# Six of eight experts of a cross-attention and expert-choice block: both batches' up projection in seven block products instead of eight

## The chip, the core and the metric

The kernel runs on one core of one Trainium2 chip. TensorE (PE, with its weight loads as PEld) multiplies, VectorE (DVE), ScalarE (ACT) and GpSimd (POOL) do elementwise work, SyncE (SP) issues transfers. The metric is device time in microseconds (us) of one execution, the median of three.

## What is computed

```python
x = x + xattn(layernorm(x), ctx, Wq, Wk, Wv, Wo, bo)      # 8 heads, 77 context rows
# then the experts, on layernorm(x); batch n = 2, tokens t = 2048, d = 512, f = 2048, 8 experts
probs = softmax(einsum('ntd,ed->nte', x, gate_w), axis=-1)
g, m = top_k(probs.transpose(0, 2, 1), 512)               # each expert takes 512 tokens of a batch
xin = x[batch_idx, m]
h = gelu(einsum('nekd,edf->nekf', xin, w1))               # the up projection
h = einsum('nekf,efd->nekd', h, w2)                       # the down projection
out = zeros.at[batch_idx, m].add(g[..., None] * h)
x = x + out
```

All of it is float32, so every large product is made of three float32r matmuls on a high and a low part of each operand: high by high, high by low, low by high.

## The kernel before

A first stage (to about 350 us) does attention, the second norm, the gates, and for batch 0 the choice of tokens. The expert stage then goes through 16 columns, one for each batch and expert, in `pe_experts`, `act_experts`, `dve_experts`, `pool_experts` and `sp_experts`. Each engine's order is written out by hand; semaphores tie them. `columns` (L1066 on) unrolls the first two columns and the last and loops over the other 13.

A column has 16 slots f, one for each chunk of 128 hidden units (KF = 16). In slot f PE does `up(f)`, 4 chunks of d by 3 matmuls of 128x512 into bank 4 + f % 2 (L1270 to L1272), and from slot 2 on `down(f - 2)`, 4 token chunks by 3 matmuls into banks 0 to 3 (L1283 to L1285). So slots 0 and 1 hold an `up` alone, and the column ends with three `down` in a row. A slot with both is 24 matmuls. ACT makes the high parts of the weights two slots ahead (L1125, L1129) and the gelu (L1147); DVE makes the low parts (L1181, L1184) and splits the gelu's result (L1200, L1202). At a column's end DVE and ACT scale two chunks of output each (L1236, L1165), and POOL adds the rows to DRAM by four indirect transfers (L1104). POOL gathers the next column's rows (L690) by a copy of their numbers (L680), and PE transposes them in slots 8, 10, 12 and 14 (L1254).

The choice of batch 1's tokens is woven into the first slots: 15 rounds of bisection, each some small DVE work (`dve_round`, L450 to L483) after the slot's split, and a small count on PE (`pe_round`, L489) after the `up` of the slot behind. `ROUNDS_AT` puts them in slots 3 to 15, 19 and 20, counted from the start of the expert stage; slots 16 to 18 (the first three of column 1) have none. Each column but the first is also looked up one column ahead: DVE makes a one-hot tile in slot 1 (`dve_one_hot`, L579), PE multiplies with it in slot 3 (`pe_lookup`, L586).

Of the kernel before, what the change touches and what calls it, by code (L numbers as in the profile page):

```python
# [4 lines left out]

# [7 lines left out]
P = 128  # L13
# [13 lines left out]
TPB = 2  # L27
# [10 lines left out]
def xattn_expert_choice(nc, x, ctx, wq, wk, wv, wo, bo, gate_w, w1, w2, out):  # L38
# [7 lines left out]
    with top:  # L46
        def sb(scope, name, shape, dt=F32):
            return scope.enter_context(nc.sbuf_tensor(name, shape, dt))
# [39 lines left out]
        grec = sb(top, "grec", [P, TPB])
        rows_in = XB[:].rearrange("p b t d -> p (b t) d")
# [3 lines left out]
        thr = sb(top, "thr", [P, E])  # L93
        cand = sb(top, "cand", [P, E, CAND])
        bits = sb(top, "bits", [P, E, CAND])
        kept = sb(top, "kept", [P, E, CAND])
        best = sb(top, "best", [P, E])
        hit = sb(top, "hit", [P, E, CAND, NT], BF16)
        cnt = sb(top, "cnt", [P, E * CAND], BF16)
        above = sb(top, "above", [P, E, NT], BF16)  # L100
        tied = sb(top, "tied", [P, E, NT], BF16)
        chosen = sb(top, "chosen", [P, E, NT], BF16)
        room = sb(top, "room", [P, E])
        chain = sb(top, "chain", [P, E, NT])
        run = sb(top, "run", [P, E, NT])
        run2 = sb(top, "run2", [P, E, NT])
        place = sb(top, "place", [P, E, NT])
        q1 = sb(top, "q1", [P, E, NT])
        q2 = sb(top, "q2", [P, E, NT])
        quarter = sb(top, "quarter", [P, E, NT])  # L110
# [1270 lines left out]
```

## Time and profile before

| | us |
|---|---|
| median of three executions (1815.7 to 1818.9) | 1816.68 |
| the profiled execution | 1814.09 |
| its span | 1812.3 |
| PE busy | 1776.3, 98% |
| PE weight loads busy | 1486.0, 82% |
| DVE busy | 957.6, 53% |
| ACT busy | 674.1, 37% |
| POOL busy | 270.4, 15% |

Matmuls are pipelined: one of 128x512 is listed with 0.39 us, but the next starts 0.23 us behind it, and this pitch is what it costs. The granted clock of TensorE is given as a share of 2.4 GHz; 0.5 is its lower level, 1.2 GHz. The profile's idle column tells how long an engine waited and for whom.

### The profile page before, as it was taken

The page shows a single profiled execution, that of the slowest core. Times are in us where ns is not written, and L with a number is a line of the kernel's source. Part 1 is how long each engine was busy: PE and PEld are TensorE (multiplying, and loading weights), DVE is VectorE, ACT ScalarE, POOL GpSimd, SP SyncE. Part 2 cuts the span into 40 slices and gives each one's busy share as a digit, 9 for nine tenths or more (in the row PEclk, how much of TensorE's full clock was granted, in tenths as well). Part 3 has the DMA queues.
Part 4 walks back from the last instruction along what each step waited for, and adds up shares of the span by engine and source line. Part 5 has one row for each costly group of instructions (what it writes and reads, how often), then busy time and mean ns, then how long its engine had stood idle before and what let it go on. Part 6 is the DMA issues. An engine that isn't in the chain of part 4 may idle for free.

```text
span 1812.3 us, 25364 instructions
## 1 busy us (share of the span) xinstructions
PE 1776.3 (98%) x8790; PEld 1486.0 (82%) x8790; DVE 957.6 (53%) x1910; ACT 674.1 (37%) x1546; POOL 270.4 (15%) x339
## 2 busy tenths in 40 slices
PE   7999999799999999999999999999999999999996
PEld 6799988687888888888888888888888888888885
DVE  5455587777665454545454545454545454444442
ACT  4556565353333333323233333333333333333321
POOL 2123222210202020202020202010111111111101
PEclk9999999899999999999999999999999999999998
DMA  3232434232525252424242525252525252424321
GB/s 122 75 135 93 139 106 175 93 129 93 139 93 140 93 139 93 139 93 139 93 139 93 140 93 148 87 154 79 164 72 168 66 172 64 167 70 161 78 85 24
DMA packets 101413, 205.87 MB, mean 114 GB/s; under 512 B 5204, under 2 KB 5358, under 8 KB 101367
## 3 DMA queue, kind: packets, MB, share of 16 engines
q1 hardware_dynamic: 87031, 171.71, 26.6%
q0 software_dynamic: 14336, 33.56, 9.8%
q8 instruction: 27, 0.44, 0.1%
q14 instruction: 19, 0.16, 0.0%
HBM read 171.70 MB, written 33.55 MB: 113 GB/s over the span
## 4 chain that ended last, share of the span: by engine, by line
PE 95%; DVE 2%; ACT 1%; POOL 1%; DMA 1%; issue 0%; SPq 0%; POOLq 0%; DVEq 0%; ACTq 0%
PE ps L1283 13%; PE ps L1270 13%; PE ps L1272 13%; PE ps L1271 13%; PE ps L1285 13%; PE ps L1284 13%; PE ps L939 4%; PE ps L940 4%; PE ps L941 4%; PE ps L1254 2%; PE ps L921 1%; PE ps L968 1%; PE ps L929 1%; PE ps L913 1%; PE ps L286 1%
## 5 line engine op out<-in xcount | busy, mean ns | idle before, releaser
L1147 ACT ACTIVATE hf<-ps 128x512 f32<-128x512 f32 x256 | 153.1, 598 | 854.8 <-PE ps L1272 854.6
L1200 DVE CAST hh<-hf 128x512 fp32r<-128x512 f32 x256 | 110.3, 431 | 599.2 <-ACT hf L1147 599.2
L1270 PE MATMUL ps<-eTh,w1h 128*128 (+1 forms) x1024 | 404.3, 395 | 0.5 <-issue 0.5
L1283 PE MATMUL ps<-w2h,hh 128*128 128x512 f32 x1024 | 401.4, 392 | 0.0
L1272 PE MATMUL ps<-eTh,w1l 128*128 (+1 forms) x1024 | 399.0, 390 | 0.0
L1285 PE MATMUL ps<-w2h,hl 128*128 128x512 f32 x1024 | 398.9, 390 | 0.0
L1284 PE MATMUL ps<-w2l,hh 128*128 128x512 f32 x1024 | 398.7, 389 | 0.0
L1271 PE MATMUL ps<-eTl,w1h 128*128 (+1 forms) x1024 | 398.6, 389 | 0.0
L1104 POOL DMA_INDIRECT out_dram<-Y,sidx x64 | 105.0, 1641 | 1080.8 <-DVE Y L1236 999.0
L1272 PEld LDWEIGHTS ps<-eTh,w1l 128*128 128x128 f32 x1024 | 192.2, 188 | 40.6
L1285 PEld LDWEIGHTS ps<-w2h,hl 128*128 128x128 f32 x1024 | 192.2, 188 | 40.3
L1283 PEld LDWEIGHTS ps<-w2h,hh 128*128 128x128 f32 x1024 | 192.4, 188 | 39.0
L1284 PEld LDWEIGHTS ps<-w2l,hh 128*128 128x128 f32 x1024 | 192.4, 188 | 38.9
L1270 PEld LDWEIGHTS ps<-eTh,w1h 128*128 128x128 f32 x1024 | 192.5, 188 | 38.6 <-issue 0.8
L1271 PEld LDWEIGHTS ps<-eTl,w1h 128*128 128x128 f32 x1024 | 192.5, 188 | 38.1
L1181 DVE TENSOR_TENSOR w1l<-w_raw,w1h 128x512 fp32r<-128x512 f32 x256 | 175.3, 685 | 30.6 <-ACT w1h L1125 30.5
L1202 DVE TENSOR_TENSOR hl<-hf,hh 128x512 fp32r<-128x512 f32 x256 | 177.4, 693 | 8.8
L1184 DVE TENSOR_TENSOR w2l<-w_raw,w2h 128x512 fp32r<-128x512 f32 x256 | 175.4, 685 | 0.0
L1129 ACT ACTIVATE w2h<-w_raw 128x512 fp32r<-128x512 f32 x256 | 160.1, 626 | 0.0
L1125 ACT ACTIVATE w1h<-w_raw 128x512 fp32r<-128x512 f32 x256 | 160.1, 626 | 0.0
L737 ACT ACTIVATE PR<-ps,nmax 128x77 f32<-128x77 f32 x256 | 78.7, 331 | 40.9 <-DVE nmax L831 40.9
L939 PE MATMUL ps<-AH,xTh 128*128 128x308 f32 (+1 forms) x256 | 80.3, 314 | 1.6 <-DVE AL L300 1.6
(159 smaller groups left out, 1716.0 us busy)
## 6 DMA issues: line engine op xcount, KB each, us to landing
w_raw<-in_L_ffn_w_dram SPq DMA_DIRECT2D x128, 1024.0 KB, 7.2
XB<-in_x_dram SPq DMA_DIRECT2D x16, 512.0 KB, 3.9
XR<-in_x_dram SPq DMA_DIRECT2D x16, 512.0 KB, 3.3
out_dram<-X SPq DMA_DIRECT2D x16, 512.0 KB, 4.6
xn_rows<-XN SPq DMA_DIRECT2D x16, 512.0 KB, 5.4
w_raw<-in_L_xattn_Wq_dram SPq DMA_DIRECT2D x1, 1024.0 KB, 8.3
w_raw<-in_L_xattn_Wo_dram SPq DMA_DIRECT2D x1, 1024.0 KB, 11.4
XB<-xn_rows,gidx POOLq DMA_INDIRECT x64
```

The costliest lines, as they stand in the source:

```text
L1125: nc.scalar.activation(w1h[:, f % SLOTS1], w1_raw[:, g % 2, :, j * P:(j + 1) * P], ACT.Copy).then_inc(f_w1h, 1)
L1129: nc.scalar.activation(w2h[:, f % SLOTS2], w2_raw[:, g % 2, j, :], ACT.Copy).then_inc(f_w2h, 1)
L1147: nc.scalar.activation(hf[:, f % 2, :], ps[:, 4 + f % 2, :], ACT.Gelu).then_inc(f_gelu, 1)
L1181: nc.vector.tensor_tensor(w1l[:, f % SLOTS1], w1_raw[:, g % 2, :, j * P:(j + 1) * P], w1h[:, f % SLOTS1].bitcast(F32), ALU.subtract).then_ ...
L1184: nc.vector.tensor_tensor(w2l[:, f % SLOTS2], w2_raw[:, g % 2, j, :], w2h[:, f % SLOTS2].bitcast(F32), ALU.subtract).then_inc(f_w2l, 1)
L1202: nc.vector.tensor_tensor(hl[:, f % 4], hf[:, f % 2, :], hh[:, f % 4].bitcast(F32), ALU.subtract).then_inc(f_h, 1)
L1270: nc.tensor.matmul(ps[:, 4 + f % 2, :], wh, flat_eTh[:, chunk], start=(k == 0), stop=False)
L1271: nc.tensor.matmul(ps[:, 4 + f % 2, :], wh, flat_eTl[:, chunk], start=False, stop=False)
L1272: last = nc.tensor.matmul(ps[:, 4 + f % 2, :], wl, flat_eTh[:, chunk], start=False, stop=(k == KD - 1))
L1283: nc.tensor.matmul(ps[:, c, :], th, wh, start=(f == 0), stop=False)
L1284: nc.tensor.matmul(ps[:, c, :], th, wl, start=False, stop=False)
L1285: last = nc.tensor.matmul(ps[:, c, :], tl, wh, start=False, stop=(f == KF - 1))
```

## The change

Experts 0 and 1 of both batches (`PLAIN`, four columns, 64 slots) go on as before, all unrolled. For experts 2 to 7 the two batches are done together. The weight block of a group of four f chunks is cut in two halves of d and two halves of f (chunk f = 2q + half), the gathered rows in two halves of d and the two batches; the result's four blocks (half of f, batch) come from seven block products in Winograd's form of Strassen's algorithm instead of eight. A product is done for q = 0 and 1, each time 2 chunks of d by 3 matmuls, so a group has 14 pieces of 6 matmuls, 84 where the same results took 96. Then all 96 matmuls of `down` follow. Six experts by four groups make 24 groups.

What is new beside the matmuls: four sums of weight blocks for each group on POOL (`w_sums`, SS1 to SS4); the high and low part of all seven left factors on ACT and DVE (`w_high`, `w_low`); for each expert four sums of row blocks on DVE (`t_stage`), their high parts on ACT (`t_high`) and low parts on POOL (`t_low`); results that PE accumulates from one product into the next are copied out between (`keep_u1`, `keep_u2`, `keep_u7` on ACT) and added on DVE (`c11`, `c22`, `c21`). Gelu is run twice for each chunk, once written as the high part and once in full (`hidden`), in place of DVE's cast. The output of a group is scaled and added to SBUF by DVE alone (`evict`), and POOL adds an expert's eight chunks to DRAM in its last group (`scatter_pair`). Buffers of the plain columns shrink from 4, 8 and 4 to 3, 5 and 3 slots. All tiles get fixed addresses. The rounds of batch 1 stand in slots 3 to 17, and all lookups in slots 24, 26, ... 50, the one-hot tile each time one slot ahead. The gather takes the row numbers directly, without a copy.

```diff
+        PLAIN = (0, 1, E, E + 1)
+        NPE = len(PLAIN) // B
+        LOOKUPS = PLAIN + tuple(b * E + e for e in range(NPE, E) for b in range(B))
...
-        SLOTS1, SLOTS2 = 4, 8
...
+        S1, S2, S3 = 3, 5, 3
...
+        A11, A12, SS2, SS3, SS1, A22, SS4 = range(NPR)
+        B11, B21, TT2, TT3, TT1, TT4, B22 = range(NPR)
+        ALPHA, BETA, GAMMA = (4, 7), (5, 0), (6, 1)
+        CHAIN = {A11: ALPHA, SS2: ALPHA, SS1: ALPHA, SS4: ALPHA, A12: BETA, SS3: GAMMA, A22: GAMMA}
+        OPENS = (A11, A12, SS3)
+        PRODUCTS = ((A11, 0), (A12, 0), (A11, 1), (A12, 1), (SS2, 0), (SS3, 0), (SS2, 1), (SS1, 0), (SS3, 1),
+                    (SS1, 1), (A22, 0), (SS4, 0), (A22, 1), (SS4, 1))
+        NU = len(PRODUCTS)
+        HIDDEN = ((0, 0), (0, 2), (1, 1), (1, 3), (0, 1), (1, 0), (0, 3), (1, 2))
...
+        W_ORDER = (A11, A12, A22, SS1, SS2, SS4, SS3)
...
+        T_AT = (54, 56, 58, 60)
...
-        ROUNDS_AT = tuple(q for q in range(3, 5 + KF) if not KF <= q < KF + LOOKUP)[:ROUNDS]
...
+        ROUNDS_AT = tuple(range(3, 3 + ROUNDS))
         CHOICE_AT = ROUNDS_AT[-1] + 1
-        assert len(ROUNDS_AT) == ROUNDS
...
+        HOT_AT = {1: 1, **{m: VALS_AT + 1 + 2 * (m - 2) for m in range(2, len(LOOKUPS))}}
+        FOUND_AT = {1: 3, **{m: VALS_AT + 2 + 2 * (m - 2) for m in range(2, len(LOOKUPS))}}
...
+            def w_sums(n):
...
+                a11, a12, a21, a22 = (w_block(n, i) for i in (A11, A12, -1, A22))
+                pool.tensor_tensor(Wf[:, SS1], a21, a22, ALU.add).then_inc(s_sum, 1)
+                pool.wait_ge(s_sum, 4 * n + 1)
+                pool.tensor_tensor(Wf[:, SS2], Wf[:, SS1], a11, ALU.subtract).then_inc(s_sum, 1)
+                pool.wait_ge(s_sum, 4 * n + 2)
+                pool.tensor_tensor(Wf[:, SS4], a12, Wf[:, SS2], ALU.subtract).then_inc(s_sum, 1)
+                pool.tensor_tensor(Wf[:, SS3], a11, a21, ALU.subtract).then_inc(s_sum, 1)
...
+                if g == G - 1:
+                    for j in range(ND):
+                        scatter_pair(x, j)
+                        if x + 1 < NS and j in (3, 5):
+                            t_low(x + 1, j // 2 - 1)
...
+                nc.scalar.activation(hhS[:, b, f], src, ACT.Gelu)
+                nc.scalar.activation(hfS[:, b, f], src, ACT.Gelu).then_inc(s_gelu, 1)
...
+            def keep_u2(n, q):
+                act.wait_ge(s_prod, NU * n + 5 + 2 * q)
+                nc.scalar.activation(u2[:, q], ps[:, ALPHA[q], :], ACT.Copy).then_inc(s_u2, 1)
...
+            def group(n):
+                x, g = divmod(n, G)
+                w2_high(n, (0, 1))
+                keep_u1(n, 0)
+                w2_high(n, (2,))
+                hidden(n, 0)
+                keep_u1(n, 1)
+                hidden(n, 1)
+                keep_u2(n, 0)
+                w2_high(n, (3,))
+                keep_u7(n, 0)
+                keep_u2(n, 1)
+                hidden(n, 2)
+                keep_u7(n, 1)
+                for m in range(3, len(HIDDEN)):
+                    hidden(n, m)
...
+            def c11(n, q):
+                dve.wait_ge(s_prod, NU * n + 2 + 2 * q)
+                dve.wait_ge(s_u1, 2 * n + q + 1)
+                nc.vector.tensor_tensor(hfS[:, 0, 2 * q], ps[:, BETA[q], :], u1[:], ALU.add).then_inc(s_c11, 1)
...
+            def product(n, m):
+                idx, q = PRODUCTS[m]
+                x, g = divmod(n, G)
+                bank = CHAIN[idx][q]
+                if q == 0:
+                    pe.wait_ge(s_Wl, NPR * n + W_ORDER.index(idx) + 1)
...
+                if idx == SS2:
+                    pe.wait_ge(s_u1, 2 * n + q + 1)
+                if idx == SS1:
+                    pe.wait_ge(s_u2, 2 * n + q + 1)
+                if idx == A22:
+                    pe.wait_ge(s_u7, 2 * n + q + 1)
+                if idx == SS4:
+                    pe.wait_ge(s_c22, 2 * n + q + 1)
+                go_on = dict(skip_group_check=idx not in OPENS)
+                for k in range(2):
+                    wh, wl = Wh[:, idx, k, q, :], Wl[:, idx, k, q, :]
+                    th, tl = Th[:, idx, k, :], Tl[:, idx, k, :]
+                    nc.tensor.matmul(ps[:, bank, :], wh, th, start=(idx in OPENS and k == 0), stop=False, **go_on)
+                    nc.tensor.matmul(ps[:, bank, :], wh, tl, start=False, stop=False, **go_on)
+                    last = nc.tensor.matmul(ps[:, bank, :], wl, th, start=False, stop=(k == 1), **go_on)
+                last.then_inc(s_prod, 1)
...
+            def group(n):
+                x, g = divmod(n, G)
+                for m in range(NU):
+                    product(n, m)
+                for j in range(2):
+                    for t in range(GF - 1):
+                        down_chunk(n, j, t)
+                for j in range(2):
+                    down_chunk(n, j, GF - 1)
+                for j in range(2, ND):
+                    if g == G - 1 and x + 1 < NS and 2 <= j < 6:
+                        t_stage(x + 1, j - 2, T_BANKS[j % 2])
+                    for t in range(GF):
+                        down_chunk(n, j, t)
```

DVE around the start of column 1. Ahead of the rows stands the work of slot 15; L1236 is the scaling that ends column 0. Before, slots 16, 17 and the first of 18:

```order
L1236 TENSOR_SCALAR Y<-ps,tok_gate 128x512 x2
L1181 TENSOR_TENSOR w1l<-w_raw,w1h 128x512
L1184 TENSOR_TENSOR w2l<-w_raw,w2h 128x512
L1200 CAST hh<-hf 128x512
L1202 TENSOR_TENSOR hl<-hf,hh 128x512
L1181 TENSOR_TENSOR w1l<-w_raw,w1h 128x512
L1184 TENSOR_TENSOR w2l<-w_raw,w2h 128x512
L1200 CAST hh<-hf 128x512
L1202 TENSOR_TENSOR hl<-hf,hh 128x512
L579 TENSOR_TENSOR hot<-row,col_iota 128x2048
```

The same place in the changed kernel, slot 16 alone:

```order
L1609 TENSOR_SCALAR Y<-ps,tok_gate 128x512 x2
L1419 TENSOR_TENSOR w1l<-w_raw,w1h 128x512
L1422 TENSOR_TENSOR w2l<-w_raw,w2h 128x512
L1436 CAST hh<-hf 128x512
L1438 TENSOR_TENSOR hl<-hf,hh 128x512
L466 SCALAR_TENSOR_TENSOR kept<-ps,cand 128x24
L469 TENSOR_REDUCE best<-kept 128x8
L471 TENSOR_TENSOR thr<-thr,best 128x8
L491 TENSOR_TENSOR cand<-thr,bits 128x24
L494 TENSOR_TENSOR hit<-probs,cand 128x384
L496 TENSOR_SCALAR bits<-bits 128x24
L499 TENSOR_REDUCE cnt<-hit 128x24
```

The round that stood in slot 19 has moved to slot 16, and the one of slot 20 to slot 17, which reads the same.

ACT in two slots of the last column before, with what it waits for:

```order
L1125 ACTIVATE w1h<-w_raw 128x512 [waits f_up,f_raw1]
L1129 ACTIVATE w2h<-w_raw 128x512 [waits f_down]
L1147 ACTIVATE hf<-ps 128x512 [waits f_h,f_up]
L1125 ACTIVATE w1h<-w_raw 128x512 [waits f_up]
L1129 ACTIVATE w2h<-w_raw 128x512 [waits f_down]
```

ACT at the start of a group in the changed kernel (u_162 is u1, u_161 u2, u_163 u7; s_prod is PE's count of products, s_c11 and s_c22 are DVE's sums):

```order
L1327 ACTIVATE v2h<-w_raw 128x512 [waits s_dn,s_raw2_0]
L1327 ACTIVATE v2h<-w_raw 128x512
L1355 ACTIVATE u_162<-ps 128x512 [waits s_c11,s_prod]
L1327 ACTIVATE v2h<-w_raw 128x512
L1345 ACTIVATE hhS<-hfS 128x512 [waits s_c11]
L1346 ACTIVATE hfS<-hfS 128x512
L1355 ACTIVATE u_162<-ps 128x512 [waits s_c11,s_prod]
L1345 ACTIVATE hhS<-hfS 128x512 [waits s_c11]
L1346 ACTIVATE hfS<-hfS 128x512
L1350 ACTIVATE u_161<-ps 128x512 [waits s_prod]
L1327 ACTIVATE v2h<-w_raw 128x512
L1360 ACTIVATE u_163<-ps 128x512 [waits s_c22,s_prod]
```

ACT now hands PE operands in the middle of the up projection, behind sums of DVE; before, it stood two slots ahead of PE with the weights and behind it with the gelu.

## Rows read from the trace of the kernel before

**Rows 1.** The page: busy us, share of the span and instructions

```profile
PE 1776.3 (98%) x8790; PEld 1486.0 (82%) x8790; DVE 957.6 (53%) x1910; ACT 674.1 (37%) x1546; POOL 270.4 (15%) x339
```

**Rows 2.** Timeline of PE, one slot (start us, us, engine, line, tiles): first `up` matmuls

```profile
1202.24 0.39 PE L1270 MATMUL ps<-eTh,w1h 128*128 x1
...
1207.68 0.39 PE L1270 MATMUL ps<-eTh,w1h 128*128 x1
```

**Rows 3.** Groups by form: busy us, mean ns, idle before and its releaser

```profile
L1202 DVE TENSOR_TENSOR hl<-hf,hh 128x512 fp32r<-128x512 f32 x256 | 177.4, 693 | 8.8
L1147 ACT ACTIVATE hf<-ps 128x512 f32<-128x512 f32 x256 | 153.1, 598 | 854.8 <-PE ps L1272 854.6
L1104 POOL DMA_INDIRECT out_dram<-Y,sidx x64 | 105.0, 1641 | 1080.8 <-DVE Y L1236 999.0 <-issue 81.8
L706 POOL TENSOR_TENSOR PR<-PR,srec 128x616 f32<-128x616 f32 x32 | 38.9, 1217 | 29.7 <-DVE srec L822 29.5
```

**Rows 4.** Timeline of PE at one of the 60 places of four transposes

```profile
1699.94 0.60 PE L1254 MATMUL ps<-ident,XB 128*128 128x128 f32 x4
1700.30 0.48 PE L1270 MATMUL ps<-eTh,w1h 128*128 x1
```

**Rows 5.** Timeline of ACT and DVE in a slot with a round: gelu, split, round

```profile
426.37 0.60 ACT L1147 ACTIVATE hf<-ps 128x512 f32<-128x512 f32 x1 [4.43 <-PE ps L1272]
427.00 0.43 DVE L1200 CAST hh<-hf 128x512 fp32r<-128x512 f32 x1 [1.80 <-ACT hf L1147]
...
428.07 0.18 DVE L450 SCALAR_TENSOR_TENSOR kept<-ps,cand 128x24 f32<-128x24 f32 x1
...
429.50 0.55 DVE L483 TENSOR_REDUCE cnt<-hit 128x24 bf16<-128x384 bf16 x1
```

**Rows 6.** Timeline at the start of column 1: gelu of slots 16 and 17, `up` of slot 18

```profile
460.71 0.60 ACT L1147 ACTIVATE hf<-ps 128x512 f32<-128x512 f32 x1 [0.99 <-PE ps L1272]
...
463.59 0.60 ACT L1147 ACTIVATE hf<-ps 128x512 f32<-128x512 f32 x1 [1.24 <-PE ps L1272]
...
463.39 0.39 PE L1270 MATMUL ps<-eTh,w1h 128*128 128x512 f32 x1
```

**Rows 7.** Timeline of DVE: the one-hot tile

```profile
555.54 2.28 DVE L579 TENSOR_TENSOR hot<-row,col_iota 128x2048 bf16<-128x2048 bf16 x1
```

**Rows 8.** Windows: us, busy of PE, PEld, DVE, ACT, POOL, granted clock, DMA

```profile
340.00:345.00 5.00, 5.00 (x12) 3.96 (x13) 2.87 (x6) 0.00 (x0) 0.00 (x0) 0.51 0.29 108
```

**Rows 9.** Timeline of PE in attention: the idle time at 340, two matmuls

```profile
339.88 0.77 PE L939 MATMUL ps<-BH,pTh 128*128 128x512 f32 x1 [3.02 <-DVE X L810]
...
346.93 0.39 PE L939 MATMUL ps<-BH,pTh 128*128 128x512 f32 x1
...
349.03 0.40 PE L939 MATMUL ps<-BH,pTh 104*128 104x512 f32 x1
```

**Rows 10.** Timeline of POOL at the first gather, and two powers behind it

```profile
346.97 0.19 POOL L680 COPY gidx<-tok_idx 128x4 uint32<-128x4 uint32 x1 [14.48 <-DVE tok_gate L601]
348.25 1.22 POOL L690 DMA_INDIRECT XB<-xn_rows,gidx  x1 [1.09 <-issue]
...
353.69 0.72 POOL L671 TENSOR_TENSOR rs<-ve,pow_c 128x2 f32<-128x2 f32 x1
...
356.86 1.23 POOL L671 TENSOR_TENSOR rs<-ve,pow_c 128x2 f32<-128x2 f32 x1
```

**Rows 11.** Timeline of DVE behind the first gather

```profile
356.85 0.69 DVE L1181 TENSOR_TENSOR w1l<-w_raw,w1h 128x512 fp32r<-128x512 f32 x1 [1.88 <-ACT w1h L1125]
```

**Rows 12.** Timeline of the kernel's end

```profile
1796.57 1.41 DVE L1236 TENSOR_SCALAR Y<-ps,tok_gate 128x512 f32<-128x512 f32 x2 [4.42 <-PE ps L1285]
...
1798.11 0.39 PE L1285 MATMUL ps<-w2h,hl 128*128 128x512 f32 x1
1798.12 1.57 POOL L1104 DMA_INDIRECT out_dram<-Y,sidx  x1 [70.60 <-DVE Y L1236]
...
1803.73 1.56 POOL L1104 DMA_INDIRECT out_dram<-Y,sidx  x1 [0.31 <-issue]
```

More of the change, by code:

```diff
@@ L100, in xattn_expert_choice @@
[L100 to L110, printed above, removed]
@@ new lines, in xattn_expert_choice @@
+        run = lookup("run", [P, E, NT])
+        run2 = lookup("run2", [P, E, NT])
+        place = lookup("place", [P, E, NT])
+        q1 = lookup("q1", [P, E, NT])
+        q2 = lookup("q2", [P, E, NT])
+        quarter = lookup("quarter", [P, E, NT])
+        row = lookup("row", [P, B, E, NT])
+        rest1 = lookup("rest1", [P, E, NT])
+        rest2 = lookup("rest2", [P, E, NT])
+        gp = [lookup(f"gp{i}", [P, E, NT], BF16) for i in range(3)]
+        inq = lookup("inq", [P, E, NT, CT], BF16)
@@ new lines, in xattn_expert_choice @@
+        W_SUMS = {SS1: 1, SS2: 2, SS4: 3, SS3: 4}
+        W_SUMS_READ = {SS1: 2, SS2: 3, SS4: 3, SS3: 4}
+        D_BANKS = (2, 3, 0)
+        ND = B * CT
+        F_ORDER = ((0, 2, 1, 3), (1, 3, 0, 2))
+        T_SUMS = (TT2, TT3, TT1, TT4)
+        T_BANKS = ((5, 6), (7, 1))
+        T_AT = (54, 56, 58, 60)
+        s_raw1 = [sem(f"s_raw1_{i}") for i in range(2)]
+        s_raw2 = [sem(f"s_raw2_{i}") for i in range(2)]
+        (s_prod, s_u1, s_c11, s_u2, s_u7, s_c22, s_c21, s_gelu, s_hid, s_sum, s_Wh, s_Wl, s_v2h, s_v2l, s_dn, s_ev, s_tr, s_Ta,
+         s_T2, s_Td, s_Th, s_Tl, s_rows, s_scat) = (sem(f"s_{n}") for n in (
+             "prod u1 c11 u2 u7 c22 c21 gelu hid sum Wh Wl v2h v2l dn ev tr Ta T2 Td Th Tl rows scat").split())
@@ L1168, in act_experts @@
             act.wait_ge(p_o, NBLK)
-            for f in range(2):
-                weights(0, f, None, None)
+            for n in range(2):
+                weights(n)
             for k in range(KD):
@@ L1173, in act_experts @@
             act_xn2T(act, NBLK - 2)
-            columns(act, body)
+            for n in range(NPL):
+                slot(n)
+                if n % KF == KF - 1:
+                    i = n // KF
+                    if i:
+                        act.wait_ge(f_scat, 16 * CT * i)
+                    for c in range(CT // 2, CT):
+                        if c < CT - 1:
+                            act.wait_ge(f_out, i * (CT - 1) + c + 1)
+                        else:
+                            act.wait_ge(f_down, n + 1)
+                        nc.scalar.activation(Y[:, c, :], ps[:, c, :], ACT.Copy,
+                                             scale=tok_gate[:, PLAIN[i], c:c + 1]).then_inc(f_ya, 1)
@@ L1246, in pe_experts @@
+            for n in range(NG):
+                group(n)
         def pe_experts(pe):
@@ L1324, in pe_experts @@
             pe_xn2T((NBLK - 2) % 2)
-            columns(pe, body)
+            for n in range(NPL):
+                slot(n)
+            for n in range(NG):
+                group(n)
         with nc.Block() as block:
```

938 lines of the change are left out of this document (630 added, 308 removed).

## The prediction

> **What bounds the kernel now.** I read the busy shares first: PE is busy 98% of the span, the next engine 53% [rows 1]. Then the timeline of PE: a slot of 24 matmuls takes from 1202.24 to 1207.68, 5.44 us, so a matmul of 128x512 costs 0.2267 us [rows 2], though it is listed with 0.39. The expert stage has 6144 such matmuls, 1392.7 us of the span; the rest of PE's time there is transposes, lookups, rounds and gates. ACT waited 854.6 us for PE's `up` [rows 3]. So PE's instruction count sets the time, and a change pays by the matmuls that it takes away, as long as nobody makes PE wait.
>
> **What it removes.** For six experts and both batches the up projection had 2304 matmuls; 24 groups by 84 are 2016. 288 fewer at 0.2267 [rows 2] is **-65.3 us**, all on the path. The down projection keeps its 1152. The Trainium skill (TensorE: Matmul & The Clock Gate, Back-to-back issue gap) gives N / 2.4 + 2.5 ns, 215.7 ns for 512 columns; by it the term would be -62.1, but the row has 226.7 and I keep the row. A group then takes 180 x 0.2267 = 40.8 us where the same work took 43.5.
>
> **Transposes.** Before, 60 places of four cost 0.36 us and 0.08 more in the matmul behind, 0.44 each [rows 4], 26.4 us. After, 12 such places and 24 of eight, about 0.87 each by the same rows doubled without the restart (4 more transposes are 0.36): 26. **0**, between -2 and +2.
>
> **The seven products: does PE wait in a group?** Let t = 0 be a group's first product; product m of the fourteen starts at 1.36 m. A result can be used 0.20 us after its matmul's pitch ends (ACT starts at 463.59 where PE went on at 463.39 [rows 6]). ACT's operation is 0.60 and the next starts 0.5 behind it; DVE's is 0.69 with 0.6 between starts [rows 3, 5]. The waits that PE has in the middle, and when they are met:
> The third pair needs u1: ACT copies it by 2.2 and 5.3; wanted at 5.44 and 8.16. SS1 with q = 0 (wanted at 9.52) needs u2: the fourth product ends at 5.44, DVE's c11 ends at 6.33, ACT's two gelus of chunk (0, 2) start at 6.4 and 6.9, the copy starts at 7.4 and ends at 8.0. That is the tightest link, **1.5 us of slack**. u2 for q = 1 is there at 10.3, wanted at 12.24; u7 at 9.0 and 13.4, wanted at 13.6 and 16.3 (q = 1, 2.9 of slack); c22 at 11.8 and 14.5, wanted at 14.96 and 17.68. The split hidden chunk that the first `down` rows need last is there at 20.4, wanted at 23.1. Behind it DVE makes three low parts and evicts the first bank at 24.7; `down` wants it at 27.2. The other low parts follow POOL's sums. A POOL sum of 512 elements I take as 1217 x 512 / 616 = 1.01 us [rows 3], four in a row from t = 19.2, so the last weight is ready by 30, and it is wanted at 47. Load in a group: ACT some 37 operations by 0.52, DVE 37 by 0.62, 19 and 23 us of 40.8. So **0** for 24 groups. Cover is the 1.5 us; if the chain ran 2 us later, each group would lose 1.
>
> **Change of expert (five times).** In the fourth group of an expert DVE gets 14 operations more and ACT 16, between the evictions. `t_stage` 1 ends on DVE at about 33.8, and PE's fourth set of transposes wants it at 35.3. POOL does `t_low` between scatters of 1.6 us [rows 3]; the second set ends 1 to 4 us into the next group, where its four results are wanted at 5.4, 6.8, 9.5 and 13.6. I take 0 and keep up to 3 us each, +15, as the other end. What could push it there: POOL slows beside DVE. A power of two elements takes 0.72 alone and 1.23 when DVE runs subtractions with both inputs in SBUF [rows 10, 11]. By that ratio (1.7) the four sums would take 7 us, and the set would still be there by 4, 6, 7 and 9. The Trainium skill (GPSIMD Engine Reference, Key points) says that GpSimd contends with VectorE's instructions that have two SBUF inputs, and the trace agrees by those two rows.
>
> **New waits in the plain columns.** Slots 16, 17, 32, 33, 48 and 49 are an `up` alone, 2.72 us. Before, no round stood in slots 16 to 18. Now DVE does one in 16 and 17, and PE's count behind the next `up` waits for it. From the gelu's start to DVE's split is 0.63, the split 1.07, the round 1.98 [rows 5]. Slot 16: the gelu starts at 460.71 [rows 6], the count is ready at 464.45, PE had been done with `up` at 463.39: **1.06**. Slot 17: DVE goes on at 464.32 with two weights (1.2), split and round until 468.63; PE is done at 467.22: **1.41**. What hides the same work elsewhere is the `down` of 2.72 us. The one-hot tile of 2.28 us [rows 7] stood in a column's slot 1 with the lookup two slots on; now slots 33 and 49 make one and PE looks up in 34 and 50: 0.20 + 0.63 + 1.07 + 2.28 + 0.06 = 4.24 after the end of `up`, against one `up` of 2.72: **1.5**, twice. Queued behind PE's wait there is `down`, and its loss is not given back. Together **+5.5**. If the clock fell each time it would cost more: at 340, after 3.02 us of idle, the granted clock was 0.51 (the level of 1.2 GHz) and 11 matmuls ran at 0.43 instead of 0.23 [rows 8, 9], 2.2 us; four times is +9. The gaps here are half as long and lie between full work; I take none.
>
> **Smaller buffers.** Three w1, five w2 and three hidden slots make ACT wait for the `up` one slot back and the `down` three back, both past when it gets there. 0, up to +2.
>
> **The first gather.** The copy at 346.97 and its wait go; the first transfer starts at 348.25 [rows 10]. PE waited 6.1 us for those rows, and POOL's norm stands behind them, so it all moves by about **-1.0** (0 to -1.3).
>
> **The end.** PE's last matmul ends at 1798.50; then come four scatters of 1.57 at a pitch of 1.87, the last from 1803.73 to 1805.3, and 7.0 more to the span's end [rows 12]. After, seven of eight are gone by then: 0.07, the eviction 0.75, 0.8 to POOL's start (as from 1797.32 to 1798.12), 1.57, 7.0: 10.2 instead of 13.8, **-3.6** (-2 to -4.5).
>
> **Addresses.** Every tile moves. No row prices an address. The nearest rows are the same matmul form at two pitches: 0.2267 in the experts and, for no reason that the trace shows, 0.2333 in attention (346.93 to 349.03 for nine [rows 9]). The new products are as the experts' in all else; I take 0, the other end is 5856 x 0.0067 = +39.
>
> **Sum.** 1814.1 (the profiled execution, 1.8 over its span) - 65.3 - 3.6 - 1.0 + 5.5 = 1749.7. It was 2.6 below the median of the runs shown, so I forecast **1752** for the median.
>
> **Rivals.** (1) The change of expert is late, by POOL or by DVE's five operations in a stage: 1 to 3 us, five times, and the four clock falls: 1759 to 1770. For it, three engines in a ring and order fixed; against it the slack above. (2) The pitch of 0.2333 holds in runs of six and three matmuls, as in attention's runs of fifteen: 1752 + 39 = 1791. Against it, `down` before also changed bank every three matmuls, at 0.2267. (3) **Slower than before**: in each group PE stops at SS1's wait for u2. It decides from 65.3 / 24 = 2.7 us per group, so the chain of c11, two gelus and copy must run 4.2 us later than worked out, twice its length. Once PE idles 3 us the clock falls: 3 + 2.2 us, 24 times, +125: 1877. For it: ACT and DVE now stand between PE's own products, and ACT has its queue of 16 gelus; against it: both are half idle. (4) The new waits don't show, since DVE runs ahead: 1746 or a little less.
>
> **Chances.** Forecast (1747 to 1758) 0.68; (4) below 1747 0.08; (1) 0.13; (2) or part of it 0.06; (3) 0.04; another way of no gain 0.01. The range leaves out the last three and half of (4): 1745 to 1768. Below a change of 0.2% a measurement of this kernel can't tell one: faster 0.95, same 0.01, slower 0.04.
>
> **What would show it.** Right: 24 stretches of about 40.8 us with PE at 98% or more and no wait of `product` on ACT or DVE in the list of waits; four waits of PE for DVE's count and one-hot tile, 1 to 1.5 us each; one scatter behind the last matmul; clock at 1.0 from 365 on. Wrong: `product` or `down_chunk` waiting in every group, a pitch of 0.2333 in the groups, the transposes of an expert change waiting for DVE, or POOL's sums at 2 us and more with low parts waited for.

## The result

| | before | changed |
|---|---|---|
| median (4 executions each) | 1816.19 | 1784.94 |
| span of the profiled execution | 1812.3 | 1783.9 |

The ratio is 0.9824, with a 95% interval of 0.9812 to 0.9836: 31 us (1.8%) faster. I had forecast 1752, in a range of 1745 to 1768, so about half of the gain that the sum promised didn't come, and the time lies above the range. The head of the changed kernel's page:

```profile
span 1783.9 us, 22943 instructions
PE 1724.9 (97%) x8502; PEld 1435.8 (80%) x8502; DVE 1164.5 (65%) x1946; ACT 807.7 (45%) x1786; POOL 477.3 (27%) x451
```

PE's busy share fell from 98% [rows 1] to 97%, and DVE's rose to 65%. To see where the time is I cut both traces at the first `up`, at the first product (before: the first `up` of column 4, at 727.14) and at the end of the last matmul:

| stretch, us | before | changed | forecast for the changed |
|---|---|---|---|
| to the first `up` | 361.84 | 362.26 | 360.8 |
| four plain columns | 365.30 | 382.69 | 379.0 |
| 24 groups (before: 12 columns) | 1071.35 | 1027.71 | 997.9 |
| from there to the span's end | 13.84 | 11.27 | 10.2 |

The two stretches of the kernel before, as windows (length, then busy time and instructions of PE, PEld, DVE, ACT, POOL, granted clock, DMA):

```profile
361.84:727.14 365.30, 365.29 (x1724) 299.58 (x1725) 216.84 (x457) 126.73 (x226) 40.02 (x37) 1.00 0.36 114
727.14:1798.49 1071.35, 1071.35 (x4961) 885.55 (x4959) 518.66 (x887) 350.44 (x641) 134.88 (x116) 1.00 0.37 113
```

The forecast for the plain columns holds the 5.5 of new waits and 8.2 that only move there from the later columns. Of these, 6.5 are 11 lookups at 0.59 each: a later column takes 89.47 in the mean, 87.04 for its 384 matmuls, 1.84 for four places of transposes, and the lookup the rest. The other 1.7 are the first joint expert's transposes in sets of eight.

29.8 of the 36.0 us between the forecast's span (1747.9) and the measured one lie in the groups. Four windows of the changed kernel, each exactly one group (engines' busy time and instructions, the granted clock behind `POOL busy`, then DMA): a plain group, the last of an expert, and the first groups of two experts.

```profile
786.35:827.71 41.36, 41.10 (x182) 33.70 (x181) 25.81 (x33) 18.06 (x33) 6.25 (x4) 1.00 0.15 51
869.10:913.47 44.37, 44.37 (x213) 37.09 (x212) 33.93 (x47) 25.83 (x48) 19.50 (x13) 1.00 0.33 72
913.47:958.19 44.72, 41.66 (x181) 33.55 (x180) 30.81 (x33) 18.45 (x35) 25.36 (x19) 1.00 0.48 118
1257.14:1304.32 47.18, 44.52 (x182) 35.43 (x180) 30.83 (x33) 18.55 (x35) 25.33 (x19) 0.93 0.45 111
```

The five last groups of an expert with their transposes take 44.37, no wait in them: 40.80 and four times 0.89. But plain groups take 41.36 instead of 40.80, and the first group of each new expert (five of them) takes 44.72, 44.72, 47.18, 45.52 and 44.72. The sums: the five first groups are 22.9 over five times 40.80, and the 13 other groups with a small gap 7.6 (0.54 to 0.60 each, one 0.85). Together that is 30.5, and transposes that cost 0.6 less in all than I had put (see "Why the prediction was wrong") give the 29.8 within 0.1. Who PE waited for (us in total, times, longest):

```profile
PE ps L1746 <- ACT u L1355: 9.2, 5, 1.9
PE ps L505 <- DVE cnt L499: 4.5, 7, 1.2
PE ps L1746 <- ACT u L1350: 3.8, 5, 0.9
PE ps L1768 <- DVE YS L1546: 3.4, 12, 0.6
PE ps L604 <- DVE hot L596: 3.3, 2, 1.7
```

L1746 is the first matmul of a product piece, L1355 and L1350 are `keep_u1` and `keep_u2`: five times each, once for every change of expert. L1768 is `down` of the group's fourth output chunk, which needs the bank that DVE's first eviction frees (L1546 here; in an expert's first group L1542, six times 0.3 at most). L604 and two of L505 are the new waits in the plain columns.

**The change of expert, read backwards.** Timelines of group 4, the first of the second joint expert (it starts at 913.47), PE, ACT, DVE and POOL (start, length, operation, idle time before it and what ended it):

```profile
921.41 0.39 PE L1748 MATMUL ps<-Th,Wl 128*128 128x512 f32 x1
923.65 0.50 PE L1746 MATMUL ps<-Th,Wh 128*128 128x512 f32 x1 [1.85 <-ACT u L1355]
...
921.96 0.63 ACT L1345 ACTIVATE hhS<-hfS 128x512 fp32r<-128x512 f32 x1 [5.71 <-DVE hfS L1513]
...
923.02 0.58 ACT L1355 ACTIVATE u<-ps 128x512 f32<-128x512 f32 x1
...
914.76 6.57 DVE L1507 TENSOR_TENSOR v2l<-w_raw,v2h 128x512 fp32r<-128x512 f32 x2 [0.34 <-ACT v2h L1327]
921.25 0.68 DVE L1513 TENSOR_TENSOR hfS<-ps,u 128x512 f32<-128x512 f32 x1
...
914.55 5.62 POOL L1209 TENSOR_TENSOR Tl<-Tf,Th 128x512 fp32r<-128x512 f32 x4
```

PE goes on when ACT has copied u1 (923.02 + 0.58). ACT copies behind the two gelus of c11. c11 (L1513) starts at 921.25, 7.8 us into the group; its inputs were there at 916.4 (two products of 1.36 into the group, and 0.2). Ahead of it in DVE's queue stand two low parts `v2l`, together 6.57 us instead of 1.3. The first of them alone is listed with 5.97: it starts 0.2 us behind POOL's four subtractions of `t_low` and ends 0.55 us behind the last of them. The whole kernel by shape (count, busy us, mean ns):

```profile
L1502 DVE TENSOR_TENSOR Wl<-w_raw,Wh 128x512 fp32r<-128x512 f32 x72 | 99.0, 1426 | 0.0
L1507 DVE TENSOR_TENSOR v2l<-w_raw,v2h 128x512 fp32r<-128x512 f32 x96 | 90.4, 962 | 56.8 <-ACT v2h L1327 56.8
L1502 DVE TENSOR_TENSOR Wl<-Wf,Wh 128x512 fp32r<-128x512 f32 x96 | 61.7, 678 | 0.0
...
L1209 POOL TENSOR_TENSOR Tl<-Tf,Th 128x512 fp32r<-128x512 f32 x48 | 69.4, 1839 | 55.8 <-ACT Th L1305 55.8
L1204 POOL TENSOR_TENSOR Wf<-w_raw 128x512 f32<-128x512 f32 x24 | 41.7, 1736 | 0.0
...
L1201 POOL TENSOR_TENSOR Wf<-Wf,w_raw 128x512 f32<-128x512 f32 x24 | 39.0, 1626 | 1.9
```

The same subtraction of 128x512 takes DVE 678 ns behind POOL's sums and 1426 in the mean beside them. **The plain group's gap** is the same thing in small (DVE, then POOL, then PE):

```profile
809.17 4.08 DVE L1502 TENSOR_TENSOR Wl<-w_raw,Wh 128x512 fp32r<-128x512 f32 x3
813.17 1.40 DVE L1546 SCALAR_TENSOR_TENSOR YS<-ps,tok_gate,YS 128x512 f32<-128x512 f32 x2
...
808.78 1.62 POOL L1203 TENSOR_TENSOR Wf<-w_raw,Wf 128x512 f32<-128x512 f32 x1
810.36 1.74 POOL L1204 TENSOR_TENSOR Wf<-w_raw 128x512 f32<-128x512 f32 x1
...
813.97 0.50 PE L1768 MATMUL ps<-v2h,hhS 128*128 128x512 f32 x1 [0.26 <-DVE YS L1546]
```

Three low parts take 4.08 instead of 2.0 while POOL sums, the eviction behind them (813.17) is late, and PE starts its next `down` 0.65 behind the last matmul instead of 0.23. The eviction comes 26.8 into the group, where I had 24.7.

**The plain columns** show the four waits of the forecast, at the places named:

```profile
463.73 0.39 PE L1641 MATMUL ps<-eTh,w1l 128*128 128x512 f32 x1
465.36 0.19 PE L505 MATMUL ps<-cnt,ones_bf 128*128 128x24 bf16 x1 [1.24 <-DVE cnt L499]
...
563.66 0.56 PE L604 MATMUL ps<-vals,hot 128*128 128x20 bf16 x16 [1.68 <-DVE hot L596]
...
565.83 0.63 PE L1652 MATMUL ps<-w2h,hh 128*128 128x512 f32 x1
```

Over the pitch they are 1.40, 1.27, 1.83 and 1.83. Behind each lookup the clock also fell to 0.5, the level of 1.2 GHz, for 3.41 us (565.83 is a matmul of 0.63 there), and 7 and 6 matmuls ran at 0.427: 2.6 us more.

### The profile page after: what moved, and what is told of

Its sections match the earlier page's. It is cut to its first block, busy times and chain, and to the rows that moved or that the text cites. A ratio compares the mean times of both kernels' runs of the same rounds, so it can differ in the third digit from the quotient of the medians.

```text
span 1783.9 us, 22943 instructions
## 1 busy us (share of the span) xinstructions
PE 1724.9 (97%) x8502; PEld 1435.8 (80%) x8502; DVE 1164.5 (65%) x1946; ACT 807.7 (45%) x1786; POOL 477.3 (27%) x451
## 4 chain that ended last, share of the span: by engine, by line
PE 77%; DVE 9%; ACT 7%; issue 6%; DMA 1%; POOL 1%; SPq 0%; DVEq 0%; ACTq 0%; POOLq 0%
PE ps L1746 7%; PE ps L1748 7%; PE ps L1747 7%; PE ps L1768 7%; PE ps L1769 7%; PE ps L1770 7%; PE ps L1652 3%; PE ps L1654 3%; PE ps L1653 3%; PE ps L1639 3%; PE ps L1641 3%; PE ps L955 3%; PE ps L1640 3%; PE ps L956 3%; PE ps L957 3%
## 5 line engine op out<-in xcount | busy, mean ns | idle before, releaser
L1768 PE MATMUL ps<-v2h,hhS 128*128 128x512 f32 x768 | 302.6, 394 | 4.9 <-DVE YS L1546 3.4
L1769 PE MATMUL ps<-v2l,hhS 128*128 128x512 f32 x768 | 299.1, 390 | 0.0
L1770 PE MATMUL ps<-v2h,hlS 128*128 128x512 f32 x768 | 299.0, 389 | 0.0
L1746 PE MATMUL ps<-Th,Wh 128*128 128x512 f32 x672 | 264.0, 393 | 13.0 <-ACT u L1355 9.2
L1748 PE MATMUL ps<-Th,Wl 128*128 128x512 f32 x672 | 263.1, 392 | 0.0
L1747 PE MATMUL ps<-Tl,Wh 128*128 128x512 f32 x672 | 263.1, 392 | 0.0
L1529 DVE TENSOR_TENSOR hlS<-hfS,hhS 128x512 fp32r<-128x512 f32 x192 | 172.3, 906 | 73.9 <-ACT hfS L1346 73.9
L1546 DVE SCALAR_TENSOR_TENSOR YS<-ps,tok_gate,YS 128x512 f32<-128x512 f32 x144 | 105.8, 745 | 113.7 <-PE ps L1770 113.7
L1768 PEld LDWEIGHTS ps<-v2h,hhS 128*128 128x128 f32 x768 | 144.2, 188 | 41.4 <-DVE YS L1546 8.4
L1746 PEld LDWEIGHTS ps<-Th,Wh 128*128 128x128 f32 x672 | 127.0, 189 | 44.0 <-ACT u L1355 11.3
L1652 PE MATMUL ps<-w2h,hh 128*128 128x512 f32 x256 | 103.4, 404 | 0.0
L1654 PE MATMUL ps<-w2h,hl 128*128 128x512 f32 x256 | 101.1, 395 | 0.0
L1653 PE MATMUL ps<-w2l,hh 128*128 128x512 f32 x256 | 101.1, 395 | 0.0
```

The source lines that it names most:

```text
L1529: nc.vector.tensor_tensor(hlS[:, b, f], hfS[:, b, f], hhS[:, b, f].bitcast(F32), ALU.subtract).then_inc(s_hid, 1)
L1546: nc.vector.scalar_tensor_tensor(out=YS[:, j], in0=src, scalar=gate, in1=YS[:, j], op0=ALU.mult, op1=ALU.add).then_inc(s_ev, 1)
L1652: nc.tensor.matmul(ps[:, c, :], th, wh, start=(f == 0), stop=False)
L1653: nc.tensor.matmul(ps[:, c, :], th, wl, start=False, stop=False)
L1654: last = nc.tensor.matmul(ps[:, c, :], tl, wh, start=False, stop=(f == KF - 1))
L1746: nc.tensor.matmul(ps[:, bank, :], wh, th, start=(idx in OPENS and k == 0), stop=False, **go_on)
```

## The experiments

The theory, A: a DVE operation whose operands lie in SBUF alone stands still while POOL runs an elementwise operation, for as long as POOL's operations follow each other; what is queued behind it on DVE (c11, an eviction) carries this to PE. The rivals: B, ACT is late at the change of expert, by its four copies for `Th`; C, DVE's queue there is simply too long.

**1. DVE's low parts of the second layer behind the sums.**

```diff
-                w2_low(n, (0, 1))
                 c11(n, 0)
-                w2_low(n, (2,))
+                c11(n, 1)
+                w2_low(n, (0, 1, 2))
                 low(n, 0)
-                c11(n, 1)
                 w2_low(n, (3,))
```

> The changed kernel with one edit in the order of DVE: the low parts of the second layer's weights (v2l) stand behind the two sums c11, not ahead of them. Theory A: an operation of DVE with both inputs in SBUF stands still while POOL runs its four subtractions for Tl back to back (v2l listed with 5.97 us instead of 0.68 at 914.76), and c11 is queued behind it. c11 has one input in PSUM and isn't held, so PE's two waits in the first group of an expert (2.02 and 1.11 us) and the clock falls behind them go: group 4 from 44.72 to 41.4, groups 12 and 16 from 47.2 and 45.5 too, 1785 to about 1765. One v2l still shows 3 to 5 us. Rival B: ACT is late (its four copies for Th end at 914.2, its copy of u1 starts at 915.16): then DVE's order changes nothing, 1784 to 1786, and group 4 stays at 44.7.

Measured 1764.77, ratio to before 0.9712 (0.9696 to 0.9728). All five first groups take 41.35 to 41.37, and the clock stays at 1.0 in the groups to the last matmul. DVE and then POOL, at the head of group 4 (913.94):

```profile
916.86 0.69 DVE L1513 TENSOR_TENSOR hfS<-ps,u 128x512 f32<-128x512 f32 x1 [1.97 <-PE ps L1747]
919.58 0.69 DVE L1513 TENSOR_TENSOR hfS<-ps,u 128x512 f32<-128x512 f32 x1 [2.03 <-PE ps L1747]
920.19 2.23 DVE L1507 TENSOR_TENSOR v2l<-w_raw,v2h 128x512 fp32r<-128x512 f32 x3
...
915.03 5.63 POOL L1209 TENSOR_TENSOR Tl<-Tf,Th 128x512 fp32r<-128x512 f32 x4
```

ACT's queue was untouched, so B falls. And c11, with one input in PSUM, runs at 0.69 in the midst of POOL's four operations. The `v2l` come when POOL is nearly done, and only 1.02 is listed for the longest, not the 3 to 5 that I expected.

**2. POOL waits for its own result between the four subtractions.**

```diff
                 for m, idx in enumerate(T_SUMS):
                     pool.wait_ge(s_Th, 4 * (2 * x + j) + m + 1)
+                    if x or j or m:
+                        pool.wait_ge(s_Tl, 4 * (2 * x + j) + m)
```

> The changed kernel with one edit on POOL: each of its four subtractions for Tl waits for the result of the one before it, so they no longer overlap (1.25 us from start to start now, about 1.7 then). Theory A1: POOL holds DVE out as long as its operations run back to back, and DVE gets a turn where POOL's pipe runs empty, as beside the weight sums, which have such waits (low parts of 1.78 us there). Then v2l at 914.8 falls from 5.97 to about 1.8, DVE reaches c11 by 918.5 instead of 921.25, both waits of PE shrink to under 0.5 us: about 1767. Theory A2: POOL always comes first, however it is spaced: v2l lasts 6 to 8 us and the kernel takes 1785 to 1790. Rival B (ACT is late): nothing changes, 1785.

Measured 1777.16, 0.9786 (0.9770 to 0.9802): between A1 and nothing. POOL's four now take 6.99 instead of 5.62:

```profile
913.20 4.77 DVE L1509 TENSOR_TENSOR v2l<-w_raw,v2h 128x512 fp32r<-128x512 f32 x2 [0.33 <-ACT v2h L1329]
...
913.82 6.99 POOL L1211 TENSOR_TENSOR Tl<-Tf,Th 128x512 fp32r<-128x512 f32 x4
```

The two `v2l` are 3.07 and 1.77 us by themselves: DVE does get in between POOL's operations, each time 0.55 us behind the end of one (917.42 and 917.96), and POOL's next one is then listed with 1.56 instead of 1.29. So the two take turns once POOL's operations don't overlap, and A2 falls. c11 starts 6.0 us into the group, not 7.8. PE's wait for u1 is gone, but that for u2 is now 1.99, and the group takes 43.8. The mechanism of A1 held and my size was too good: I had counted 1.8 for the first low part too.

**3. The first two evictions ahead of the low parts.**

```diff
+                evict(n, 0)
+                evict(n, 1)
                 if more:
                     for idx in W_ORDER[0:3]:
                         w_low(n + 1, idx)
-                evict(n, 0)
-                evict(n, 1)
```

> The changed kernel with one edit in the order of DVE: the evictions of the first two down banks stand ahead of the three low parts Wl from w_raw, not behind them. Theory A: these three take 4.08 us instead of 2.0 beside POOL's weight sums and end at t = 26.8 of a group, so that the first eviction lets PE go on 0.42 us late (0.65 between starts), in 18 groups. Evictions read PSUM and aren't slowed. The gap at t = 27.0 goes and a plain group takes 40.8 to 40.9 instead of 41.36: 1785 to 1775 or 1776. The first groups of an expert keep their 3.1 us. If the gap is only the eviction's own length behind PE's last matmul of that bank, it stays and so does the time.

Measured 1764.37, 0.9710 (0.9694 to 0.9726), 11 us better than expected. The gap 27 us into a group (t = 27.0) is gone everywhere:

```profile
784.08:824.88 40.80, 40.80 (x181) 33.80 (x180) 23.71 (x33) 18.06 (x33) 5.80 (x4) 1.00 0.16 52
910.06:953.26 43.20, 41.37 (x181) 33.63 (x180) 27.78 (x33) 18.44 (x35) 23.55 (x19) 1.00 0.46 120
```

The 13 plain groups give 7.6 us, as expected. The first groups give 11 (45.4 in the mean to 43.2), of which I had expected only the small gap's 2.8: POOL starts its four subtractions 0.1 us into the group instead of 1.1, PE's first wait is then 1.04 instead of 2.02, and the clock doesn't fall. The shift comes through POOL's scatters, which wait for evictions. In both traces the scatter ahead of POOL's first four subtractions starts 0.28 us behind the end of its eviction, and this eviction starts 10.6 us ahead of group 4 instead of 9.6, since the low parts ahead of it take 0.68 each. Another 1.4 us is a clock fall in the plain columns that this execution didn't have.

**4. POOL copies instead of summing.** Four lines of the form

```diff
-                pool.tensor_tensor(Wf[:, SS1], a21, a22, ALU.add).then_inc(s_sum, 1)
+                pool.tensor_copy(Wf[:, SS1], a21).then_inc(s_sum, 1)
```

> The changed kernel in which POOL's four weight sums are copies of one operand (the second operand is left out, so six of the seven products have other weights than they should; same size, same waits). Theory A says that POOL holds DVE out only with two inputs in SBUF: then the low parts Wl from w_raw fall from a median of 1.78 us to 0.68, the gap at t = 27.0 of a plain group goes and the kernel takes about 1775. If any operation of POOL in SBUF does it, the low parts stay between 1.2 and 1.8 and the time at 1785.

Measured 1763.58 in one execution. Copies are shorter, but a condition of two inputs on POOL's side is not what decides:

```profile
L1502 DVE TENSOR_TENSOR Wl<-w_raw,Wh 128x512 fp32r<-128x512 f32 x72 | 67.5, 989 | 0.0
...
L1201 POOL COPY Wf<-Wf 128x512 f32<-128x512 f32 x24 | 23.0, 957 | 1.5
...
L1199 POOL COPY Wf<-w_raw 128x512 f32<-128x512 f32 x24 | 14.9, 620 | 649.3 <-PE ps L1748 649.3
```

DVE's low parts beside the copies are 1.09 each (46 of 72), not 0.68, and a copy on POOL that meets one is 0.96 instead of 0.62. So both my alternatives were half wrong: one input is enough to shut DVE out, but the time is set by POOL's own length (0.62 for a copy, 1.29 for a sum). Plain groups are 40.80: with DVE's order untouched the small gap goes when POOL's operations are shorter. First groups are 43.05, and the kernel 11 us faster than expected, as in experiment 3.

**5. Lookups of slots 33 and 49 read two slots later.**

```diff
+        for m in range(2, len(LOOKUPS)):
+            if HOT_AT[m] % KF == 1:
+                FOUND_AT[m] += 1
```

> The changed kernel with one edit in the schedule of the plain columns: the two lookups whose one-hot tile is made in slots 33 and 49 are read by PE two slots later (35 and 51), not one. My account of these slots: DVE's chain (gelu, split, one-hot of 2.28 us) is longer than the one up (2.72) that covers it; PE waits 1.83 us there twice and the clock falls to 0.5 behind each (3.41 us long, 7 and 6 matmuls at 0.427). Both gaps and both falls go: -3.7 for the waits, -2.6 for the falls, 1785 to about 1778.5; the groups stay at 41.36 and 44.7. Rival: the wait only moves to the next reader, or the clock falls there for the short stretch without down (five lookups and ups in a row), not for the gap: then 1783 to 1785.

Measured 1776.95, 0.9778 (0.9763 to 0.9793). The plain columns go from 382.69 to 375.88, -6.8 against the expected -6.3; no wait of PE is left in them behind slot 18, and the clock stays at 1.0 over both places. The groups are as before.

**6. The round first in slots 16 and 17.** `split` is the gelu's split as before, now a function.

```diff
             def slot(n):
+                if n in (KF, KF + 1):
+                    dve_round(dve, 1, ROUNDS_AT.index(n))
+                    weights(n + 2)
+                    if n == KF + 1:
+                        split(n - 1)
+                        split(n)
+                    return
```

> The changed kernel with one edit in the order of DVE in slots 16 and 17: the threshold round comes first, then the weights, and the two splits of the hidden chunk last (down wants them only from slot 18 on). By my account PE's two waits for the count (1.40 and 1.27 us over the pitch, at 463.7 and 468.0) go or fall under 0.3 together: 1785 to 1782.4. Rival: the late splits make down of slots 18 and 19 wait, or ACT's gelu of slot 18 (it waits for the split of 16), and the time stays within 1 us of 1785.

Measured 1781.47, 0.9807 (0.9792 to 0.9822), which looks like the forecast, but the trace says that the rival is half true. Both waits for the count are gone, and there is one new one behind them:

```profile
464.65 0.19 PE L505 MATMUL ps<-cnt,ones_bf 128*128 128x24 bf16 x1
466.57 0.50 PE L1662 MATMUL ps<-w2h,hh 128*128 128x512 f32 x1 [1.73 <-DVE hl L1436]
```

`down(16)` waits for the split that I had put last. 2.67 us of waits became 1.69, so the edit is worth 1.0. The rest of the 3.5 us can't be put down to it: the clock fell behind one lookup instead of two (1.4 us), and the first `up` stands at 359.97, where the other kernels, with the same code up to there, have 361.3 to 363.1.

**7. The low parts Tl on DVE instead of POOL.** `t_low` becomes a function of DVE's with the same waits; the first set stands ahead of `evict(n, 5)`.

```diff
-                        if x + 1 < NS and j in (3, 5):
-                            t_low(x + 1, j // 2 - 1)
...
                 x, g = divmod(n, G)
+                if x and g == 0:
+                    t_low(x, 1)
                 w2_low(n, (0, 1))
                 c11(n, 0)
...
+                    t_low(x + 1, 0)
```

> The changed kernel in which DVE, not POOL, makes the low parts Tl at a change of expert, the second set at the head of the new expert's first group, ahead of v2l and c11. It puts 2.4 us more work in DVE's queue ahead of c11, and takes POOL's 5.6 us away. Theory A (POOL shuts DVE out): v2l is back at 0.68 everywhere, c11 starts at about t = 4.7 instead of 7.8, PE's waits of 2.02 and 1.11 us go with their clock falls: group 4 at 41.4 to 41.8, 1785 to about 1765 to 1767. Rival C (DVE's queue is simply too long at the change of expert): with 2.4 us more in it the waits grow to 4 or 5 us and the kernel takes 1795 or more.

Measured 1764.08, 0.9711 (0.9696 to 0.9726). The first groups take 41.45 to 41.47. With 2.4 us more work in DVE's queue ahead of c11 the wait disappears, so C falls, and the operation that had lasted 5.97 is back (counts and mean ns as above):

```profile
L1511 DVE TENSOR_TENSOR v2l<-w_raw,v2h 128x512 fp32r<-128x512 f32 x96 | 63.9, 686 | 55.2 <-ACT v2h L1325 55.2
L1505 DVE TENSOR_TENSOR Tl<-Tf,Th 128x512 fp32r<-128x512 f32 x40 | 24.8, 677 | 0.0
```

DVE does in 0.68 us what POOL does in 1.25 (from start to start) or more.

**8. A copy in the place of DVE's subtraction.**

```diff
-                    nc.vector.tensor_tensor(v2l[:, f], w2_raw[:, n % 2, f, :], v2h[:, f].bitcast(F32),
-                                            ALU.subtract).then_inc(s_v2l, 1)
+                    nc.vector.tensor_copy(v2l[:, f], w2_raw[:, n % 2, f, :]).then_inc(s_v2l, 1)
```

> The changed kernel in which DVE's low parts v2l are plain copies of w_raw (the subtraction of the high part is left out, so the down products have other weights than they should). It asks what DVE's operation must be like to stand still beside POOL. If it takes two inputs in SBUF: the copy at the head of group 4 runs in its normal 0.3 to 0.7 us while POOL makes its four low parts, c11 comes in time, group 4 takes 41.4 and the kernel 1765. If any operation of DVE that touches only SBUF is shut out: the copy lasts 5 to 6 us, group 4 stays at 44.7 and the kernel at 1785.

Measured 1780.06 in one execution. DVE at the head of group 4 (913.43), POOL, and DVE's same copy when POOL is done:

```profile
914.71 6.04 DVE L1507 CAST v2l<-w_raw 128x512 fp32r<-128x512 f32 x2 [0.33 <-ACT v2h L1327]
...
921.27 0.41 DVE L1507 CAST v2l<-w_raw 128x512 fp32r<-128x512 f32 x1
...
914.49 5.63 POOL L1209 TENSOR_TENSOR Tl<-Tf,Th 128x512 fp32r<-128x512 f32 x4
```

A copy with one input, from SBUF to SBUF, stands still just the same: 5.70 instead of 0.41. Group 4 takes 44.24.

**9 and 10. The edits together.** The first version has the edits of 1, 3, 5 and 6; the second also changes slot 17:

```diff
                     dve_round(dve, 1, ROUNDS_AT.index(n))
+                    if n == KF + 1:
+                        split(n - 1)
                     weights(n + 2)
                     if n == KF + 1:
-                        split(n - 1)
                         split(n)
```

> The changed kernel with four edits of order together: v2l behind the two sums c11, the first two evictions ahead of the low parts Wl, lookups of slots 33 and 49 read two slots later, rounds first in slots 16 and 17. If each works by itself as its own run shows or should (-20, -10, -6.3, -2.6): 24 groups at 40.8, no wait of PE for a product, clock at 1.0 from 365 to the last matmul, and 1785 - 38.9 = 1746. If order moves the waits elsewhere instead, 1750 to 1765.

> The version with four edits of order, and in slot 17 DVE's split of slot 16 ahead of the weights. In the version before it PE's only wait behind 365 is down(16) for that split, 1.69 us over the pitch at 467.6; the split now ends 1.2 us earlier, so 0.5 us is left: 1748.2 to about 1747. If up(19) then waits for its weights instead, no gain.

Measured 1748.20, 0.9621 (0.9608 to 0.9634), and 1746.02, 0.9612 (0.9599 to 0.9625). In the first, the windows of two groups (the second is the first of an expert), and then all that PE waited for from its first `up` to its last matmul (the 1.0 is at that first `up`):

```profile
778.90:819.70 40.80, 40.80 (x182) 33.78 (x180) 23.46 (x33) 18.07 (x33) 5.80 (x4) 1.00 0.15 52
904.87:945.67 40.80, 40.80 (x181) 33.78 (x180) 23.43 (x33) 18.57 (x35) 23.57 (x19) 1.00 0.48 127
```

```profile
PE ps L1664 <- DVE hl L1439: 1.7, 1, 1.7
PE ps L1651 <- issue: 1.0, 1, 1.0
```

All 24 groups together take 997.2 us, 0.7 under the forecast's figure, with not one wait. The second version cuts the 1.69 to 0.47, but a count then waits 0.39: the plain columns are 0.75 shorter (375.09 to 374.34), and another 1.7 us between the two profiled executions is where the first `up` stands. The second version is 70 us under the kernel before, and 39 of these come from the order of instructions alone.

## Why the prediction was wrong

**Matmuls: right.** 288 fewer at 0.2267, and groups of 40.80 where nothing waits. (The down projection keeps 2304 matmuls, 24 by 96; the 1152 in the prediction are one batch's. The sum doesn't use them.) **Addresses: right** to take none, the groups have the pitch of 0.2267 (rival 2 falls). **Transposes:** a set of eight costs 0.89 where I had 0.87, and a place of four 0.46 where I had 0.44, so that all of them together went from 27.6 to 27.0: -0.6 for my 0.

**The step that failed is "does PE wait in a group: 0"**, with the change of expert. Its chain of times is right where POOL is quiet (in a plain group ACT copies u2 from 7.4 to 8.0, to the tenth as forecast), and it even names one of the places: PE waits before SS2 for u1 and before SS1 for u2, and the second is what the prediction called the tightest link. What is wrong is one duration, DVE's 0.69 for every subtraction. I had seen POOL and DVE disturb each other, in the power that took 1.23 instead of 0.72 [rows 10], and read it as a ratio (1.7) that only slows POOL. It was a queue: that power started 0.01 behind DVE's subtraction of 0.69 [rows 11] and ended 0.55 behind the subtraction's end (356.85 + 0.69 + 0.55 = 358.09 = 356.86 + 1.23). Whoever comes second waits for the first. It is the only one of the 32 powers before that met a subtraction with both inputs in SBUF, and 1.23 is the only length over 0.72, so a single row carried either reading. Read as a queue, it works in the other direction too, and POOL's operations in this kernel are long and come four at a time. Beside it my size for a sum on POOL was off: 1.29 alone and 1.63 to 1.74 beside DVE, not 1.01.

The price, in the profiled execution: PE's waits of 2.02 and 0.8 to 1.1 us in five groups, with the clock falls behind two of them, 20 us; the late first eviction 0.4 of wait and 0.56 in all, in 18 groups, 10 us. Experiments 1 and 7 give the first back (20.2 and 20.9 between medians), experiment 3 the second, and 8 us of the first with it. Rival (1) had the right place and named POOL, with 3 us each at most; the groups lost 4.0 each, and 0.56 more by the late eviction.

The Trainium skill has it (SBUF — State Buffer, Who interferes with whom): GpSimd and a DVE instruction with two SBUF inputs, or a copy or cast in a two-port mode, hold the shared ports exclusively, and the second one fully blocks. The runs agree: 5.97 and 5.70 for operations of 0.68 and 0.41, and nothing for c11 with an input in PSUM; no row names the mode of the cast. I had drawn on the Trainium skill's softer word (GPSIMD Engine Reference, Key points), contention.

**The plain columns: mechanism right, sizes off.** 6.3 us of waits for 5.5 (1.40, 1.27, 1.83, 1.83 for 1.06, 1.41, 1.5, 1.5). The clock falls that I set aside came behind the two lookups, 2.6 us, taken back by experiment 5; not behind the counts. The stretch was 3.7 over my figure: 0.8 in the waits, 2.6 in the falls, and 0.3 that I can't place.

**The first gather:** PE's wait for it went from 6.12 to 5.24 us, 0.9 of my 1.0, but the first `up` is not earlier (362.26 and 361.84). That point moves by up to 3 us between kernels that are the same up to it, so a term of 1 us there can't be checked. **The end:** 11.27 instead of 10.2. DVE and POOL came as forecast:

```profile
1772.70 0.75 DVE L1546 SCALAR_TENSOR_TENSOR YS<-ps,tok_gate,YS 128x512 f32<-128x512 f32 x1 [1.97 <-PE ps L1770]
...
1773.73 1.55 POOL L1189 DMA_INDIRECT out_dram<-YS,tok_idx  x1 [1.17 <-DVE YS L1546]
```

But from this last scatter's end to the span's end it is 8.66 us, where it was 7.0 behind four in a row [rows 12]. Why stays open.

## What to carry to other kernels

When a change gives elementwise work to POOL, take it that DVE's subtractions and casts within SBUF stand still for as long as POOL's operation lasts, and where POOL's follow each other without a wait for their own results, for the whole run of them (0.68 became 5.97 here), and look what stands behind them in DVE's queue. Put first in that queue what the busiest engine waits for and what reads PSUM (evictions, sums from a bank); the low parts can come late. And where a row shows an operation lengthened beside another engine's, check whether its end follows the other's end by a fixed time before reading it as a ratio.

## What the runs showed of the hardware

- POOL and DVE shut each other out in SBUF. DVE's subtraction of 128x512 ended 0.55 us behind the end of POOL's operation each time (806.99 and 807.54, 808.70 and 809.25; in experiment 2, 915.71 and 916.27).
- Four POOL operations that don't wait for each other's results start 1.25 us apart though listed with 1.87, and held DVE out for 5.6 us as if they were one. With a wait of POOL for its own result between them DVE got its turn: 3.07 and 1.77 instead of 5.97.
- DVE operations with one operand in PSUM kept their 0.67 to 0.75 beside POOL's: 10 evictions and 22 sums of rows in the changed kernel, and ten c11 in experiment 1.
- The clock: PE's gap of 2.06 us at a lookup in slots without `down` was followed by the lower level in the changed kernel both times, and only once of two in some of the other runs; waits of 2.0 and 1.1 us close together in five groups were followed by it in two of them here, and in three with the edits of experiments 5 and 6. The wait of 2.0 us that stands alone in the five groups of experiment 2 never was, nor the waits of 1.0 and 1.1 in those of experiment 3, nor the gaps of 1.6 us for the counts.
